# A four-stage fp32 transformer kernel: its written-out order of units, and their PSUM banks, replaced by another order and other banks

## The chip, the cores and the metric

One core of one Trainium2 chip. The metric is the device time in microseconds of one execution. The kernel before took 571.74, 571.04 and 569.04 us in three runs, median 571.04. All data is fp32.

## The reference

16 samples, each an image of 3 x 128 x 128 and a text of 32 tokens x 192. The image becomes 64 patches of 16 x 16 (768 numbers) and these tokens of 192. Three parts follow; `_layernorm` is without gain where none is given.

```python
# part 1, 64 image tokens per sample
x = layernorm(patches @ patch_w + patch_b) * g + b + positions
identity = x
x = sparse_attn(ff(x)) + identity        # ff = gelu(y @ ff1) @ ff2 (192 -> 768 -> 192); 12 heads of 16, window 64
x = ff(x) + x
h = concatenate([x, txt], axis=1)        # 96 tokens per sample
# part 2, y = layernorm(h)
y = y + (silu(conv4(xb)) * silu(z)) @ out_proj      # xb, z = halves of ln(y) @ in_proj
y = y + attn(ln(y)) @ attn_proj                     # 12 heads of 16 over 96 tokens
y = y + gelu(ln(y) @ ffn1) @ ffn2
h = h + y
# part 3, y = layernorm(h)
q, k, v = y @ qkv                        # 12 heads of 64, q and k normalised per head
o = softmax(q k / 8) v * gate(y)         # gates: 2 shared and 10 experts, the 2 highest kept
return h + o @ proj
```

## The kernel before, in words

The 16 samples are taken in 4 groups of 4. A group's 256 image tokens are 2 tiles of 128, its 384 tokens of all kinds are 3. The work of a group is cut into three chains, each a sequence of units: **a** is part 1 and the first branch of part 2 (the convolution), **b** is attention and feed-forward of part 2, **c** is part 3. Chain a of group 0 has buffers of its own and is written **d**; chain c of group 2 likewise, written **e**. A unit is one product of TensorE and what the other engines do with it. `STEPS_TEXT` (lines 70 to 103) names all 403 units in the order in which they are issued, as `name.k:group=bank`: `b_s.0:3=2` is the scores of the first sample set of group 3, in PSUM bank 2 and the two behind it. Some names that the text uses below:

- a_em: patches times weights (24 matmuls; needs x_in, a 768 KB load by SyncE, L623 for group 1, L643 for groups 2 and 3). a_x0: its transpose. a_f1 and a_f2: feed-forward, gelu on ScalarE (L1253). a_qk, a_v, a_s, a_pt, a_o, a_ot, a_pr: attention. a_in, a_cv, a_gt, a_out: the convolution branch, a_cv and a_gt without TensorE.
- b_u: transpose of the normalised tokens; its statistics are DVE's, the inverse root GpSimd's (L1931), the result `u` DVE's (L1611). b_qk, b_v: q, k and v. b_s: scores; DVE takes the maximum (L1715) and subtracts it, ScalarE takes the exponential (L1366, L1371). b_pt: the transposed probabilities, after DVE has divided (L1729, L1741). b_o, b_pr: the rest of attention. b_f1, b_f2: feed-forward.
- c_g: the gates (some 25 small DVE instructions). c_qk: q and k of one tile, normalised per head on DVE (L1828 to L1839) and GpSimd (L1983). c_qt: their transposes. c_v, c_s, c_pt, c_o, c_pr as in b.
- b_e, b_n, a_e, c_e, c_n and the like are parts of a softmax on ScalarE and DVE, without TensorE. a_bc, a_tb, a_pb and a_wc prepare biases and one weight. warm.0 to warm.3 are matmuls whose result nobody reads (L1220).

`run` (L527) goes through the order once per engine: TensorE, ScalarE, DVE and GpSimd each issue their part of every unit in the order of the text, and SyncE the loads of a_em and of the text of a_ht. So the place of a unit in the text is its place in each of these queues. There is no other planner.

PSUM has 8 banks. `BANKS` (L124) gives the number of neighbouring banks of each kind of unit: 3 for a_f1, a_in, b_qk, b_s, b_pt, b_f1, c_qk, c_qt, c_s and c_pt, 2 for a_qk, a_s, a_pt, b_u, b_v, c_v and c_o, 1 for the others. `PsumPlaces` (L165) takes the bank of the text where one is given (173 units before), and else the banks that have gone unused for longest. `reads_before` (L507) makes TensorE wait ahead of a unit until all that was in its banks has been read, by the counts in `READ_BY` (L129):

```python
"b_s": lambda k: [("b_sub", 3 * k + 3), ("b_exp", 2 * k + 1)],   # L129 ff.
```

Every wait on data is ahead of the unit's first matmul too:

```python
pe.wait_ge(w.S["x_in"], w.upto("x_in", w.a))                     # a_em, L774 ff.
for sem_read, value in reads_before(w, ("a_em", 0)):
    pe.wait_ge(sem_read, value)
```

`narrow_first_units` (L189) decides from the order for 23 units in which sequence their wide and narrow matmuls come; it gives 23 units with either text.

## Time and profile before

| | |
|---|---|
| three runs, us | 571.74, 571.04, 569.04 |
| profiled execution, span, us | 569.6 |
| TensorE busy (PE) | 515.9 us, 91%, 4673 matmuls |
| weight loads (PEld) | 396.6 us, 70% |
| VectorE busy (DVE) | 406.6 us, 71%, 891 instructions |
| ScalarE busy (ACT) | 299.0 us, 52%, 488 instructions |
| GpSimd busy (POOL) | 97.0 us, 17%, 85 instructions |
| DMA | 16.02 MB, nearly all in the first 60 us |

The span is the time from the first to the last instruction of one profiled execution, here 569.6 us, the execution's own time as far as the profile gives one; the three runs lie at most 2.1 us above it and 0.6 below. PE, DVE, ACT, POOL and SP are the five engines; PEld are the weight loads, which run beside the matmuls. "Granted clock" or PEclk is TensorE's clock as a share of 2.4 GHz.

### The profile page before, as it was taken

The numbers are of one execution on the slowest core, as the hardware profiler recorded it, in microseconds if no ns is written. First come the engines' busy times: TensorE is split into PE (matmuls) and PEld (weight loads), VectorE is DVE, ScalarE is ACT, GpSimd is POOL, SyncE is SP. The second block draws the span as 40 slices with busy tenths as digits, with TensorE's granted clock in tenths as the row PEclk, the third lists the DMA queues.
The fourth block names the chain that finished last, engine by engine and source line by source line (L and its number), as shares of the span: only waits on it lengthen the run. The fifth ranks groups of instructions, "written<-read, shape, count | busy, mean of one in ns | idle before, by whom it ended". The sixth has DMA issues, their size and how long they took to land.

```text
span 569.6 us, 11352 instructions
## 1 busy us (share of the span) xinstructions
PE 515.9 (91%) x4673; PEld 396.6 (70%) x4673; DVE 406.6 (71%) x891; ACT 299.0 (52%) x488; POOL 97.0 (17%) x85
## 2 busy tenths in 40 slices
PE   5799989898999999999999999999969798989696
PEld 5576667677887566786976667777945677686475
DVE  4234877688777957779768857869749688748982
ACT  0125446356338546858346546866335568525762
POOL 6022400100320422110010422100010231011200
PEclk9799999979999999999999999999998999999999
DMA  9995020000000000100000000000000000000000
GB/s 215 287 203 142 17 63 0 8 2 2 0 2 1 2 1 2 57 8 2 1 22 1 3 1 0 1 1 1 2 22 1 1 2 2 1 22 1 1 1 22
DMA packets 12675, 16.02 MB, mean 28 GB/s; under 512 B 6235, under 2 KB 10048, under 8 KB 12240
## 3 DMA queue, kind: packets, MB, share of 16 engines
q1 hardware_dynamic: 9712, 12.71, 9.4%
q10 hardware_dynamic: 2400, 2.00, 1.1%
q0 software_dynamic: 512, 0.59, 0.6%
q8 instruction: 37, 0.61, 0.5%
q14 instruction: 14, 0.11, 0.1%
HBM read 14.11 MB, written 1.18 MB: 27 GB/s over the span
## 4 chain that ended last, share of the span: by engine, by line
PE 70%; DVE 17%; ACT 7%; issue 3%; POOL 1%; DMA 1%; ACTq 0%; DVEq 0%; POOLq 0%
PE ps L692 16%; PE ps L1005 9%; PE ps L702 8%; PE ps L682 7%; PE ps L825 4%; PE ps L783 3%; DVE smax L1715 3%; DVE pr L1741 3%; PE ps L1066 2%; PE ps L1180 2%; DVE psum L1729 2%; PE ps L1202 2%; PE ps L1156 2%; PE ps L1056 2%; PE ps L840 2%
## 5 line engine op out<-in xcount | busy, mean ns | idle before, releaser
L1715 DVE TENSOR_REDUCE smax<-ps 96x12 f32<-96x1152 f32 (+1 forms) x28 | 37.8, 1351 | 18.1 <-PE ps L1056 10.8
L1729 DVE TENSOR_REDUCE psum<-pr 128x12 f32<-128x1152 f32 (+1 forms) x24 | 32.3, 1344 | 4.3 <-ACT pr L1371 4.3
L1366 ACT ACTIVATE pr<-ps,less 128x96 f32<-128x96 f32 (+1 forms) x96 | 24.6, 337 | 17.9 <-DVE less L1717 17.8
L1409 ACT ACTIVATE squares<-ps 128x1536 f32<-128x1536 f32 x12 | 17.4, 1450 | 27.5 <-PE ps L702 21.6
L1957 POOL TENSOR_TENSOR side_wide<-attn,w_mask 128x1024 f32<-128x1024 f32 (+1 forms) x12 | 20.7, 1748 | 59.1 <-ACT attn L1261 47.4
L1828 DVE TENSOR_REDUCE ss<-squares 128x24 f32<-128x1536 f32 x12 | 21.0, 1749 | 12.1 <-ACT squares L1409 12.1
L1983 POOL TENSOR_TENSOR squares<-squares,qk_root 128x512 f32<-128x512 f32 x8 | 16.7, 2082 | 75.0 <-DVE qk_root L1504 75.0
L1931 POOL TENSOR_TENSOR ln_root<-ln_root,minus_half 128x3 f32<-128x3 f32 x8 | 6.8, 856 | 129.5 <-DVE ln_root L1603 129.5
L682 PE MATMUL ps<-w_cqkv,side_c 64*96 64x384 f32 (+1 forms) x96 | 27.4, 500 | 0.0
L1005 PE MATMUL ps<-w_ff,b_kB 128*128 128x192 f32 x144 | 25.5, 329 | 0.0
L692 PE MATMUL ps<-w_cqkv,side_c 128*128 128x512 f32 (+1 forms) x72 | 25.0, 492 | 0.0
L1005 PEld LDWEIGHTS ps<-w_ff,b_kB 128*128 128x128 f32 x144 | 23.2, 190 | 0.5 <-issue 0.2
L1253 ACT ACT_TABLE_LOAD x7 | 9.0, 1283 | 26.6 <-PE ps L702 26.5
L1720 DVE TENSOR_TENSOR pr<-ps,smax 128x768 f32<-128x768 f32 (+1 forms) x24 | 22.8, 949 | 0.0
L1076 PE MATMUL ps<-w_ident,pr 128*96 128x128 f32 x144 | 18.0, 275 | 3.8 <-issue 2.4
L1376 ACT ACTIVATE side_qk<-ps 96x1536 f32<-96x1536 f32 x12 | 17.2, 1444 | 7.6 <-PE ps L1076 7.5
L1371 ACT ACTIVATE pr<-pr 128x768 f32<-128x768 f32 (+1 forms) x24 | 20.4, 852 | 0.0
L1076 PEld LDWEIGHTS ps<-w_ident,pr 128*96 128x96 f32 x144 | 15.2, 126 | 6.9 <-issue 3.9
L1005 PE MATMUL ps<-w_cproj,b_kB 128*128 128x192 f32 x108 | 19.3, 329 | 0.7 <-ACT b_kB L1441 0.7
L1056 PE MATMUL ps<-b_kB,heads 32*32 32x192 f32 x576 | 15.8, 360 | 4.6 <-ACT b_kB L1345 3.1
L692 PEld LDWEIGHTS ps<-w_cqkv,side_c 128*128 128x128 f32 x72 | 13.0, 190 | 9.9 <-issue 9.3
L1931 POOL TENSOR_TENSOR x_root<-x_root,minus_half 128x6 f32<-128x6 f32 (+1 forms) x6 | 6.5, 1091 | 73.9 <-DVE x_root L1606 37.5
(360 smaller groups left out, 1356.8 us busy)
## 6 DMA issues: line engine op xcount, KB each, us to landing
x_in<-in_xT SPq DMA_DIRECT2D x3, 768.0 KB, 4.5
b_kB<-in_cqkv SPq DMA_DIRECT2D x1, 1152.0 KB
w_cqkv<-in_cqkv SPq DMA_DIRECT2D x1, 864.0 KB
out<-side_c ACTq DMA_DIRECT2D x3, 288.0 KB, 2.3
w_cqkv<-in_cqkv SPq DMA_DIRECT2D x1, 855.0 KB
heads<-in_xT ACTq DMA_DIRECT2D x3, 256.0 KB, 3.8
side_in<-in_patchT SPq DMA_DIRECT2D x3, 192.0 KB, 4.4
side_tok<-in_tok_ff SPq DMA_DIRECT2D x2, 288.0 KB, 6.9
```

What stands on the lines that cost most here:

```text
L682: m = pe.matmul(out_ap, lhs(n, kc, r), rhs(n, kc, r), start=opens and banks[n] not in banks[:n], stop=closes and banks[n] not in banks[n + ...
L692: m = pe.matmul(out_ap, lhs, rhs, start=opens and bank not in [x[0] for x in wide[:n]], stop=closes and bank not in [x[0] for x in wide[n ...
L702: m = pe.matmul(out_ap, lhs(half, r), rhs(half, r), start=opens and part == 0, stop=closes and part == 1)
L825: m = pe.matmul(t[:, 0:TA], w_tff2[:, kc, 0:128], w.x.a_h[:, kc, :], start=(n == 0), stop=(n == F // 128 - 1))
L1005: m = pe.matmul(t[:, 0:D], lhs[:, kc, tile * 128:(tile + 1) * 128], rhs[:, kc, :], start=(kc == 0), stop=(kc == n_k - 1))
L1056: m = pe.matmul(t[32 * of:32 * of + 32, bank, second * 2 * N:(second + 1) * 2 * N], b_qT[r, c, at:at + 32], b_kBv[r, :, c, of * N:(of + 1) ...
L1076: m = pe.transpose(t[0:N, h // 4, h % 4 * 128:(h % 4 + 1) * 128], pr_all[:, s % 2, h * N:(h + 1) * N], w_ident[:, :])
L1366: m = act.activation(e[:, s % 2, h * N:(h + 1) * N], t[0:rows, h // 4, h % 4 * N:(h % 4 + 1) * N], ACT.Exp, scale=head ** -0.5, bias=less[ ...
L1715: dve.tensor_reduce(mx, t, AX.X, ALU.max).then_inc(w.S[stage + "_sub"], 1)
L1720: dve.tensor_tensor(e[:, s % 2, 0:DVE_LESS * N].rearrange("p (b h k) -> p b h k", b=b, k=N), t[:, 0:b], mx[:, 0:b].unsqueeze(3).to_broadca ...
L1729: dve.tensor_reduce(psum[0:rows, s % 2, :], e, AX.X, ALU.add).then_inc(w.S[done], 1)
L1828: dve.tensor_reduce(ss[:, :], sq.rearrange("p (h d) -> p h d", d=HD2), AX.X, ALU.add)\
```

## The change

Only the text of the order changes. It names the same 403 units, in another order, and 307 of them have a bank where 173 had. The whole text is replaced; these are the stretches of which the prediction speaks, in each of them the lines before (-) and after (+).

```diff
 STEPS_TEXT = """
-    d_en:0 d_em:0=7 a_bc=7 d_x0:0=7 d_f1.0:0=1 a_en:1 a_em:1=4 d_f2.0:0=5 d_h2.0:0=2 a_x0:1=4 d_qk:0=5 a_f1.0:1=2
-    d_v:0=6 d_e.0:0 d_s.0:0 a_f2.0:1=3 a_h2.0:1=6 d_pt.0:0 d_s.1:0 d_e.1:0 a_qk:1 d_o.0:0 d_pt.1:0=0 a_tb=5 d_ot.0:0
-    d_o.1:0 a_wc.0 warm.2 a_pb d_ot.1:0=2 a_e.0:1 d_pr:0=0 a_s.0:1=6 a_wc.1 d_f1.1:0=3 a_e.1:1 a_s.1:1=0 d_f2.1:0
-    d_h2.1:0 warm.1 d_ht:0=3 a_pt.0:1 a_v:1=6 a_o.0:1 d_u:0 a_pt.1:1 a_wc.2 d_in.0:0=2 a_ot.0:1 a_o.1:1=1 a_ot.1:1=7
...
-    d_out.1:0=7 d_out.2:0 a_f2.1:1=1 a_h2.1:1=5 b_u.1:0=3 a_ht:1 b_qk:0 a_u:1 b_e.0:0 b_s.0:0 b_s.1:0 b_e.1:0 b_v:0
-    b_n.0:0 b_n.1:0 a_in.0:1 b_pt.0:0=3 b_s.2:0 b_e.2:0 b_n.2:0 b_pt.1:0=3 a_in.1:1 b_pt.2:0=3 b_o.0:0 b_o.1:0=0
-    b_o.2:0=3 b_o.3:0=7 a_cv.0:1 a_cv.1:1 a_cv.2:1 a_gt.0:1 a_gt.1:1 b_pr.0:0=3 a_gt.2:1 b_pr.1:0 b_pr.2:0=2
-    a_em:2=0 a_out.0:1 a_out.1:1=1 b_u.2:0 a_out.2:1 b_f1.0:0=1 a_en:2 b_f1.1:0 b_u.1:1 a_wc.3 a_x0:2 b_f2.0:0
...
-    a_gt.0:2 c_pr.0:0 c_o.2:0=5 c_pt.3:0 a_gt.1:2 a_cv.2:2 c_pr.1:0=4 c_o.3:0=5 a_gt.2:2 a_out.0:2=7 a_out.1:2=1
-    a_out.2:2=4 a_em:3=3 b_u.1:2=5 a_en:3 c_pr.2:0=7 c_u:1 b_qk:2 b_v:2=6 a_x0:3 b_s.0:2=2 b_s.1:2 b_e.0:2 b_n.0:2
-    b_e.1:2 b_n.1:2 warm.3 a_f1.0:3 a_f2.0:3 a_h2.0:3=7 b_pt.0:2=1 b_s.2:2 b_e.2:2 b_n.2:2 a_qk:3=2 a_v:3=0 c_g:1=1
...
-    a_out.0:3=3 a_out.1:3=0 a_out.2:3=3 e_u:2=4 c_pr.2:1=3 b_u.1:3 b_qk:3=1 b_s.0:3=2 b_s.1:3 b_n.0:3 b_e.0:3 b_v:3
-    b_e.1:3 e_v.0:2=3 b_n.1:3 b_pt.0:3 b_s.2:3 b_e.2:3 b_n.2:3 e_qk.0:2=5 b_pt.1:3 b_pt.2:3 b_o.0:3=6 b_o.1:3
-    b_o.2:3 b_o.3:3 b_pr.0:3 b_pr.1:3=5 b_pr.2:3 e_v.1:2=0 e_g:2=4 b_u.2:3=0 e_qt.0:2 e_qk.1:2 e_qk.2:2=5 b_f1.0:3
...
-    c_v.0:3 c_qt.0:3=2 c_qt.1:3 c_s.0:3=0 c_e.0:3 c_s.1:3=5 c_n.0:3 c_e.1:3 c_n.1:3 c_qt.2:3 c_v.1:3=3 c_pt.0:3
...
+    d_en.0:0 d_em.0:0=3 warm.2:0=7 warm.1:0=2 a_bc.0:0=1 d_x0.0:0=5 a_em.0:1=7 d_f1.0:0=2 a_en.0:1 a_x0.0:1=0
+    d_f2.0:0=1 d_h2.0:0=7 a_f1.0:1=4 d_qk.0:0=1 a_f2.0:1=0 a_h2.0:1=1 d_e.0:0 d_s.0:0=6 d_v.0:0=5 a_qk.0:1=0 d_s.1:0=2
+    d_pt.0:0=4 d_e.1:0 d_o.0:0=0 d_pt.1:0=2 a_tb.0:0=4 d_ot.0:0=1 d_o.1:0=3 d_ot.1:0=7 a_pb.0:0=0 d_pr.0:0=6 a_e.0:1
+    a_s.0:1=0 a_wc.0:0 d_f1.1:0=3 a_e.1:1 a_s.1:1=0 d_f2.1:0=2 d_h2.1:0=3 warm.0:0=0 warm.3:0=4 d_ht.0:0=1 a_v.0:1=0
...
+    a_pr.0:1=4 d_gt.0:0 d_cv.1:0 d_cv.2:0 a_em.0:2=3 d_gt.1:0 d_gt.2:0 a_f1.1:1=4 a_en.0:2 d_out.0:0=0 d_out.1:0=7
+    d_out.2:0=3 a_f2.1:1=4 a_h2.1:1=2 b_u.1:0=6 a_ht.0:1=1 b_qk.0:0=5 a_u.0:1=1 b_e.0:0 b_s.0:0=4 b_s.1:0=0 b_e.1:0
+    b_n.0:0 b_n.1:0 a_in.0:1=5 b_pt.0:0=3 b_s.2:0=0 b_e.2:0 b_v.0:0=4 a_in.1:1=1 b_pt.1:0=5 b_n.2:0 b_pt.2:0=0
+    a_cv.0:1 a_cv.1:1 b_o.0:0=4 b_o.1:0=2 a_gt.0:1 a_gt.1:1 a_cv.2:1 a_gt.2:1 b_o.2:0=4 b_o.3:0=5 b_pr.0:0=1
+    b_pr.1:0=6 b_pr.2:0=7 a_out.0:1=1 a_out.1:1=7 b_u.2:0=4 a_x0.0:2=3 a_out.2:1=2 a_wc.2:0 b_f1.0:0=5 b_f1.1:0=0
...
+    b_pt.2:1=0 a_pt.1:2=5 c_g.0:0=7 b_o.0:1=6 b_o.1:1=1 b_o.2:1=2 b_o.3:1=0 b_pr.0:1=5 c_qt.0:0=2 c_qt.1:0=5
+    b_pr.1:1=0 b_pr.2:1=1 c_v.1:0=2 a_ot.0:2=6 a_o.1:2=1 b_u.2:1=2 a_ot.1:2=4 c_s.0:0=5 c_s.1:0=1 a_pr.0:2=0
+    a_em.0:3=7 c_n.0:0 c_e.0:0 c_e.1:0 c_n.1:0 a_en.0:3 c_qk.2:0=0 a_f1.1:2=4 b_f1.0:1=0 b_f1.1:1=5 a_f2.1:2=1
...
+    a_out.0:2=5 a_out.1:2=2 a_out.2:2=5 c_pr.2:0=3 b_u.1:2=5 a_x0.0:3=2 b_qk.0:2=4 a_f1.0:3=0 c_u.0:1=3 a_f2.0:3=7
+    b_s.0:2=1 b_e.0:2 a_h2.0:3=0 b_n.0:2 c_qk.0:1=5 c_qk.1:1=0 a_qk.0:3=4 b_v.0:2=6 b_pt.0:2=0 b_s.1:2=3 b_s.2:2=0
+    b_e.1:2 a_v.0:3=5 b_e.2:2 b_n.1:2 b_n.2:2 c_v.0:1=3 a_s.0:3=5 b_pt.1:2=0 a_e.0:3 c_g.0:1=7 b_pt.2:2=2 a_s.1:3=0
+    a_pt.0:3=5 b_o.0:2=2 b_o.1:2=5 b_o.2:2=7 a_e.1:3 b_pr.0:2=6 b_pr.1:2=5 b_o.3:2=4 a_o.0:3=6 a_pt.1:3=4 c_qt.0:1=0
...
+    a_out.2:3=2 e_u.0:2=6 c_pr.2:1=2 b_u.1:3=0 e_g.0:2=7 b_qk.0:3=2 e_qk.0:2=5 e_qk.1:2=2 b_v.0:3=0 e_qt.0:2=5
+    b_s.0:3=0 b_s.1:3=3 b_n.0:3 b_e.0:3 b_e.1:3 b_n.1:3 e_v.0:2=6 e_v.1:2=0 e_qt.1:2=2 b_pt.0:3=5 b_s.2:3=0 b_e.2:3
+    b_n.2:3 e_qk.2:2=4 b_pt.1:3=0 b_pt.2:3=5 e_s.0:2=0 b_o.0:3=7 e_s.1:2=3 e_n.0:2 e_e.0:2 b_o.1:3=7 e_e.1:2 e_n.1:2
...
+    c_g.0:3=6 c_qk.0:3=3 c_qk.1:3=0 c_qk.2:3=5 c_qt.0:3=1 c_qt.1:3=5 c_s.0:3=0 c_e.0:3 c_s.1:3=5 c_v.0:3=3 c_e.1:3
...
     """
```

A unit written without `.k` or with `.0` is the same unit.

## Rows read from the trace of the kernel before

**Rows 1.** The page, part 1: TensorE, busy us, share, instructions.
```profile
PE 515.9 (91%) x4673; PEld 396.6 (70%) x4673; DVE 406.6 (71%) x891; ACT 299.0 (52%) x488; POOL 97.0 (17%) x85
```

**Rows 2.** The page, part 4: the chain that ended last, by engine.
```profile
PE 70%; DVE 17%; ACT 7%; issue 3%; POOL 1%; DMA 1%; ACTq 0%; DVEq 0%; POOLq 0%
```

**Rows 3.** Windows: length, busy us of PE, PEld, DVE, ACT, POOL; PEclk; DMA share; GB/s.
```profile
17.47:24.30 6.83, 5.72 (x15) 4.45 (x16) 0.92 (x3) 0.00 (x0) 0.00 (x0) 0.50 1.09 268
...
113.05:119.87 6.82, 6.82 (x110) 5.08 (x89) 5.43 (x8) 4.63 (x12) 0.00 (x0) 0.50 0.01 2
...
427.07:430.48 3.41, 3.41 (x20) 2.33 (x12) 3.34 (x6) 1.76 (x5) 0.00 (x0) 0.50 0.00 0
```

**Rows 4.** The same view, stages between two starts.
```profile
75.78:112.84 37.06, 33.18 (x262) 25.59 (x263) 27.33 (x74) 16.89 (x30) 3.49 (x3) 1.00 0.10 27
...
186.00:235.00 49.00, 45.32 (x410) 33.14 (x410) 35.46 (x93) 28.00 (x37) 16.80 (x10) 1.00 0.06 18
...
281.32:345.00 63.68, 60.13 (x621) 44.78 (x621) 46.20 (x108) 32.45 (x56) 14.34 (x11) 1.00 0.02 6
...
416.50:456.00 39.50, 30.89 (x382) 22.30 (x383) 26.87 (x50) 20.09 (x34) 2.94 (x2) 0.96 0.03 9
...
456.00:509.71 53.71, 49.85 (x454) 40.27 (x454) 41.35 (x95) 32.90 (x50) 9.32 (x6) 1.00 0.01 2
...
509.71:569.60 59.89, 48.33 (x427) 35.24 (x425) 42.32 (x94) 31.40 (x46) 6.24 (x3) 1.00 0.03 11
```

**Rows 5.** One source line, the load of x_in: issue and landing.
```profile
L623 SPq DMA_DIRECT2D x_in<-in_xT x1: 432/432/432, 10.3 to 10.3; - x1
...
DMA to landing us min/median/max: 12.2/12.2/12.2
```

**Rows 6.** Timeline: start, length, engine, line, operation [idle before <-releaser]; PE, the start.
```profile
18.28 0.42 PE L745 MATMUL ps<-w_ident,squares 128*128 128x128 f32 x1
...
26.22 4.17 PE L783 MATMUL ps<-side_in,x_in 128*128 128x192 f32 x24
...
30.22 1.03 PE L825 MATMUL ps<-side_qk,side_tff 128*128 128x256 f32 x4
```

**Rows 7.** Timeline, PE: the wide part of a_f1.0:3.
```profile
299.40 2.83 PE L692 MATMUL ps<-x0T,side_tok 128*128 128x256 f32 x12 [0.82 <-ACT pr L1366]
```

**Rows 8.** Timeline, ACT: the gelu table behind d_f1.0.
```profile
26.46 1.28 ACT L1253 ACT_TABLE_LOAD   x1 [26.46 <-PE ps L702]
```

**Rows 9.** Timeline, 112 to 146 us, PE, ACT and DVE.
```profile
112.84 3.37 PE L1056 MATMUL ps<-b_kB,heads 32*32 32x192 f32 x96 [1.36 <-DVE b_kB L1705]
...
116.29 1.04 ACT L1366 ACTIVATE pr<-ps,less 128x96 f32<-128x96 f32 x4 [1.61 <-DVE less L1717]
...
123.22 1.47 PE L1076 MATMUL ps<-w_ident,pr 128*96 128x128 f32 x12
...
140.54 4.06 PE L783 MATMUL ps<-side_in,x_in 128*128 128x192 f32 x24
...
144.58 0.96 DVE L1611 TENSOR_SCALAR u<-pT,ln_mv,ln_root 128x192 f32<-128x192 f32 x3 [0.96 <-POOL ln_root L1931]
```

**Rows 10.** Timeline, 282 to 286 us, PE and DVE.
```profile
282.29 4.06 PE L783 MATMUL ps<-side_in,x_in 128*128 128x192 f32 x24
...
284.83 0.96 DVE L1611 TENSOR_SCALAR u<-xr,x_mv,x_root 128x192 f32<-128x192 f32 x3 [0.96 <-POOL x_root L1931]
```

**Rows 11.** Timeline, PE, b_s and b_v of group 3.
```profile
425.18 2.34 PE L1056 MATMUL ps<-b_kB,heads 32*32 32x192 f32 x96 [2.66 <-ACT b_kB L1345]
...
427.45 3.79 PE L682 MATMUL ps<-w_qkv,bT 128*96 128x192 f32 x16
```

**Rows 12.** Timeline, DVE in the tail: c_g, c_qk and the first maximum.
```profile
513.03 0.20 DVE L1775 TENSOR_REDUCE gsm<-ps 96x4 f32<-96x40 f32 x1 [1.72 <-PE ps L682]
...
518.68 1.75 DVE L1828 TENSOR_REDUCE ss<-squares 128x24 f32<-128x1536 f32 x1
...
534.18 1.35 DVE L1715 TENSOR_REDUCE smax<-ps 96x12 f32<-96x1152 f32 x1 [0.17 <-PE ps L1180]
```

More of the change, by code:

```diff
@@ L81 @@
-    a_h2.0:2 b_pt.0:1 b_s.2:1 a_v:2 b_n.1:1 b_e.2:1 a_qk:2=6 c_v.0:0=1 b_n.2:1 c_g:0 b_pt.1:1=3 b_pt.2:1=0 a_s.0:2=6
-    b_o.0:1=2 b_o.1:1=3 b_o.2:1=4 b_o.3:1 a_e.0:2 a_s.1:2=2 a_pt.0:2 b_pr.0:1=4 b_pr.1:1 a_e.1:2 a_o.0:2 a_pt.1:2=2
-    b_pr.2:1=6 a_ot.0:2=3 a_o.1:2=2 c_qk.0:0=4 a_ot.1:2=0 c_qk.1:0=1 a_pr:2=6 c_qt.0:0=3 c_qk.2:0 a_f1.1:2=3
-    c_qt.1:0 a_f2.1:2=7 b_u.2:1=4 a_h2.1:2 c_s.0:0=3 c_s.1:0 c_n.0:0 c_e.0:0 c_v.1:0 c_e.1:0 c_n.1:0 b_f1.0:1
-    b_f1.1:1=0 a_ht:2 b_f2.0:1=7 c_pt.0:0 b_f2.1:1=6 c_qt.2:0=2 a_u:2 b_f2.2:1 c_o.0:0=1 c_pt.1:0=3 c_s.2:0 c_e.2:0
@@ L91 @@
-    a_e.1:3 b_o.3:2=0 a_o.0:3=7 a_pt.1:3=1 b_pr.2:2 a_ot.0:3=5 a_o.1:3=6 c_qk.0:1 a_ot.1:3 c_qk.1:1=5 c_v.0:1 a_pr:3
-    c_qt.0:1=4 c_qk.2:1 a_f1.1:3 c_qt.1:1=0 a_f2.1:3=6 b_u.2:2 c_s.0:1=0 c_s.1:1 a_h2.1:3=3 c_n.0:1 c_e.0:1 c_e.1:1
-    b_f1.0:2=0 b_f1.1:2 c_n.1:1 a_ht:3 c_qt.2:1 c_v.1:1 c_pt.0:1 a_u:3 b_f2.0:2=5 c_o.0:1 c_pt.1:1 c_s.2:1 c_e.2:1
-    c_s.3:1=0 c_e.3:1 c_n.2:1 c_v.2:1=6 c_n.3:1 a_in.0:3=3 b_f2.1:2=0 c_o.1:1=4 c_pt.2:1 c_v.3:1=4 a_in.1:3 a_cv.0:3
-    a_cv.1:3 a_cv.2:3 c_pr.0:1 a_gt.0:3 b_f2.2:2=0 a_gt.1:3 c_o.2:1=6 c_pt.3:1=2 c_pr.1:1=5 a_gt.2:3 c_o.3:1
@@ L105 @@
+    c_o.1:3=1 c_e.3:3 c_v.3:3=3 c_pr.0:3=1 c_pt.2:3=4 c_o.2:3=6 c_pt.3:3=0 c_n.3:3 c_pr.1:3=5 c_o.3:3=6 c_pr.2:3=1
     """
```

25 lines of the change are left out of this document (16 added, 9 removed).

## The prediction, made before the changed kernel ran

> **What bounds the kernel now.** I read the page from the top. TensorE is busy for 515.9 of 569.6 us, 91%, and the chain that ended last lies on it for 70% of the span, on VectorE for 17% [rows 1, 2]. So the time is TensorE's work plus its holes, 569.6 - 515.9 = 53.7 us, plus what a lower clock adds inside the busy time. The granted clock is at its lower level (0.50, which is 1.2 GHz) in three stretches, 17.06 us in all: 17.47 to 24.30, 113.05 to 119.87 and 427.07 to 430.48 us [rows 3]. The windows then tell where the holes are [rows 4]: 3.88 us in 75.78 to 112.84 (37.06 less 33.18), 3.68 in 186 to 235, 3.55 in 281 to 345, 8.61 in 416.5 to 456, 3.86 in 456 to 509.71 and 11.56 in the tail. In the tail VectorE is busy for 42.32 of 59.89 us and takes the maximum only 0.17 us after its last work [rows 4, 12]: there it is VectorE that sets the pace.
>
> The change leaves every matmul in place, so 515.9 us stay but for the clock. What can change is the cover of each wait: how much TensorE work stands between a product and the next unit that needs its result back from ScalarE, VectorE, GpSimd or a DMA. I went through the new order unit by unit with the durations and latencies of before. The sum goes against the profiled execution's 569.6 us, which is 1.4 us under the median 571.04; I add the difference to the median.
>
> **A, the start (15 to 76 us): +3.0 us.** The new order puts a_em of group 1 ahead of d_f1.0. It reads x_in, whose DMA is issued at 10.3 us and takes 12.2 us, so it lands at 22.5 [rows 5]. TensorE is at that point when d_x0 ends, 18.28 + 0.42 = 18.7 us, where before a_em came at 26.22 without a wait [rows 6]. From 22.5: a_em 4.06 (its length at full clock [rows 10]), then d_f1.0 of 2.83 us for its wide part [rows 7] and 1.5 for the narrow one, end 30.9. Then ScalarE must load the gelu table, 1.28 us [rows 8], and make the first tile, 0.5, and only a_x0 (0.6) stands in between: d_f2.0 starts near 32.9 where it started at 30.22 [rows 6], +2.7. The clock: before, TensorE was near idle from 13.84 until the fall at 17.47. Now 1.6 us of warm matmuls stand in that hole, but two holes follow, so I expect a stretch at half clock over a_em as well: at most the 6.83 us of before [rows 3], adding between 0 and 2.5 us; I take 1.3. Against it go the warm matmuls, moved into a hole (-1.6), and the 0.9 us wait ahead of d_qk. d_o.0 and d_ot.1 now stand directly behind d_pt.0 and d_o.1: +1.5. Sum 2.7 + 1.3 - 1.6 - 0.9 + 1.5 = 3.0, from 1.6 to 4.3.
>
> That d_f1.0 can't slip past a waiting a_em: in the trace every matmul behind a wait starts after it [rows 9, 11]. The Trainium skill ("TensorE: Matmul & The Clock Gate", Part 2, Step-by-step) says the same, only weight loads are pulled ahead; if matmuls could pass, A would be about -1. The Trainium skill's page "DMA: Bandwidth & Descriptors" (Specifications) gives about 358 GB/s per core; here the load stretch shows 268 GB/s with the DMA engines all busy [rows 3]. By the page x_in would land, as an estimate, a quarter sooner (near 17 us), there would be no stall, and A would be about -1 too; the trace has the landing itself, so I keep 22.5.
>
> **B (76 to 112): -0.8 us.** a_em of group 2 comes here, as cover ahead of a_f1.1, and two warm matmuls cover d_ht. Of 3.88 us of holes [rows 4] I see about 0.8 covered; bounds -1.5 and -0.2.
>
> **C (112 to 148): +3.0 us.** First, a_in.0:1 is placed in banks 5 to 7, and b_s.0:0 in 4 to 6. So it waits until the exponentials of b_s.0:0 have been read: the first four end at 116.29 + 1.04 = 117.33, b_s itself ends at 112.84 + 3.37 = 116.21, and the last follow within a microsecond [rows 9]. +1.2 to 1.9. Then b_pt.0:0 has only a_in.0 (3.3) where b_v stood as well; it started at 123.22, 7.0 us after b_s ended [rows 9], and now would have 1.5 + 3.3 = 4.8 us plus b_s.1's own part: +1.0. Second, a_em:2 stood at 140.54 for 4.06 us [rows 9] between b_pr and b_u.2, whose input u comes at 144.58 + 0.96 = 145.54 off GpSimd's root [rows 9]. b_pr ended as a_em began; a_out.0 and a_out.1 give 2.1 us of cover. 145.5 - 140.5 - 2.1 = 2.9, and the gates that a_out needs are as late: +3.2. Third, b_v and a_in.1 now stand between b_s.2, b_pt.1 and b_pt.2, where 1.7 us of holes were: -1.4. VectorE works on during the first stall, so part of the second is paid: -1.4. 2.6 + 3.2 - 1.4 - 1.4 = 3.0; from 1 (the clock doesn't fall, b_v is 1.8 us shorter) to 5.
>
> **D (148 to 235): -0.7 us.** 3.68 us of holes in 186 to 235 [rows 4]; in the new order c_qk and c_v stand between b's and a's softmax units and I count about 3 left, with one new bank handover (c_qt.1:0 in bank 5 behind b_pr.0:1). From -3 (all gone) to +0.5.
>
> **235 to 281: 0.** 0.3 us of holes before; nothing to gain.
>
> **E (281 to 345): +2.2 us.** a_em:3 stood at 282.29 for 4.06 us with u ready at 284.83 + 0.96 [rows 10]. It is moved 45 us ahead. a_out.2 to b_u.1 took 3.7 us and 2.1 remain as cover: +1.6, b_qk:2 +0.5. Two handovers (a_v:3 in bank 5 behind b_s.1:2, a_o.0:3 in 6 behind b_pr.0:2) cost up to 1.5 and 1.4 by the exponentials' latency above; I take half, +1.5. Of the 3.55 us of holes [rows 4] 1.4 go. From 0 to +4.
>
> **F (345 to 416.5): -0.9 us.** The smallest term: two TensorE waits, 0.3 us ahead of b_f1.0:2 and 1.2 ahead of c_qt.2:1, get a unit before them; from -2.2 to 0.
>
> **G (416.5 to 509.71): -3.9 us.** Before, b:3 runs with little beside it: b_s.0:3 waits 2.66 us, and b_v behind it, from 427.45, runs for 3.03 of its 3.79 us at half clock, which costs half of that, 1.5 [rows 3, 11]. The new order puts e_g, e_qk.0 and e_qk.1 (9.7 us of matmuls) ahead of b_s.0:3. Gone: 2.66, 1.5 of clock, 0.9 ahead of b_pt.0, and 1.5 each ahead of b_pt.2 and b_o.0, 8.1 together. New: VectorE takes 518.68 - 513.03 = 5.65 us for c_g and (534.01 - 518.68) / 3 = 5.1 for each c_qk [rows 12], so 15.9 us for e_g and two e_qk, while TensorE has 18 us of work until b_s.0:3 ends, so the maximum starts hardly late; later stages with e_s, e_pt and e_o lose cover, and I count 4.2. Bounds: -7 (half of the 12.5 us of holes and the clock) and +3 (rival 2).
>
> **Tail: 0 +- 0.3.** c_v.0:3 moves behind c_s.1:3. VectorE has no hole there [rows 12], so a TensorE hole that is filled gives nothing back.
>
> **Sum.** 3.0 - 0.8 + 3.0 - 0.7 + 0 + 2.2 - 0.9 - 3.9 + 0 = +1.9. Profiled: 571.5; on the median 572.9 us. What a measurement of this kernel tells from no change is 0.5%, 2.9 us; so this is "within 0.5%", just.
>
> **Rivals.**
> 1. *The cover is spread better than my gap count shows* (0.31). G gives -7, D -3, F -2, and A and C stay at their lower ends, 1.6 and 1: with B -0.8 and E +2.2 the sum is -8.0, 563.0 us; with half of those differences about 568. For it: the largest holes, in 416 to 456 [rows 4], get 9.7 us of matmuls, and a clock that doesn't fall there. Against: units that lose cover in C and E.
> 2. *VectorE becomes the bound in b:3* (0.15). It takes its units in the same order, and e_g's and two e_qk chains stand ahead of b_s.0:3's maximum. If they take over the 18 us that TensorE has (the root and the products on GpSimd come back late), b's softmax, the longest chain of G, starts late by all of it, and TensorE stands at b_pt.0:3. It decides from 18 us on; at 22 us G is about +3 and the sum +8.8: 579.8 us.
> 3. *The start at half clock and the lost covers at their upper ends* (0.2): A 4.3, C 5, E 4: sum +7.3 on top of G -3.9 and the rest as above less 0.4, 578 us.
> 4. *Banks decide nothing and stalls move only* (part of my forecast, 0.34): TensorE's holes after are as many as before, in other places. That the kernel does other work than before is excluded: the same 403 units, the same shapes.
>
> My range for 8 in 10: 563 to 581, which takes in rival 1's end and rival 2. The likeliest one alone spans 569 to 576. Chances from the cases: faster by over 0.5% 0.31, within 0.5% 0.34, slower by over 0.5% 0.35 (rivals 2 and 3).
>
> **What would show it.** A: a hole before a_em:1 that ends at 22.5 with x_in's DMA named, and d_f2.0 near 32.9 or later. C: a hole at a_in.0:1 released by ScalarE's exponentials, and one ahead of b_u.2:0 released by DVE u. E: a hole of 1 to 2 us ahead of b_u.1:2. G: no clock fall near 427 and b_s.0:3 without a wait; a maximum that starts over 2 us after it would be rival 2. I am wrong if A shows no wait for x_in, if 416 to 510 keeps 12 us of holes, or if new waits come in D to F that are not named here.

## The result, and the profile after

The changed kernel takes 585.14 us (584.68 to 585.30 in four runs) where the kernel before, beside it, took 571.39: a ratio of 1.0237 (95%: 1.0193 to 1.0281), slower by 13.7 us. The forecast was 572.9 us, 563 to 581; the time lies outside that range.

The first view is part 1 and part 4 of the page (they answer to [rows 1, 2]). All line numbers are 3 higher than before, as the text of the order is 3 lines longer (in most runs below they are 4 or 5 higher).

```profile
PE 522.7 (90%) x4673; PEld 400.4 (69%) x4673; DVE 404.9 (69%) x891; ACT 293.8 (50%) x484; POOL 95.7 (16%) x85
...
PE 57%; DVE 23%; issue 8%; ACT 5%; POOL 3%; DMA 2%; SPq 2%; ACTq 0%; DVEq 0%; POOLq 0%
```

TensorE's busy time has grown by 6.8 us (522.7 less 515.9) with the same 4673 matmuls, and the span by 13.6 (583.2 less 569.6), so the holes have grown by 6.8 as well. The chain lies on TensorE for 57% of the span where it was 70%, on VectorE for 23% where it was 17%, and 8% of it is "issue", time in which the engine waited for nothing that the profile shows.

Where in the span that lies is shown by windows cut at the same two units in both kernels, the starts of b_u.1:3 and of c_u:3 (before, then the changed kernel; the tail of before is the last line of [rows 4]):

```profile
0.00:416.54 416.54, 386.87 (x3416) 298.82 (x3416) 296.09 (x654) 214.60 (x358) 78.47 (x74) 0.98 0.15 36
416.54:509.71 93.17, 80.74 (x833) 62.56 (x834) 68.19 (x144) 52.99 (x84) 12.26 (x8) 0.98 0.02 5
```

```profile
0.00:426.43 426.43, 386.73 (x3416) 298.07 (x3416) 294.47 (x654) 210.91 (x355) 77.22 (x74) 0.97 0.14 35
426.43:520.00 93.57, 83.66 (x833) 63.77 (x834) 68.05 (x144) 49.98 (x82) 12.21 (x8) 0.96 0.02 5
520.00:583.20 63.20, 52.33 (x427) 38.60 (x425) 42.37 (x94) 32.92 (x47) 6.24 (x3) 0.92 0.03 10
```

Up to b_u.1:3 the loss of 9.9 us is holes alone (29.7 us before, 39.7 after). Behind it the holes have shrunk, by 2.5 us in G and 0.7 in the tail, and TensorE's busy time has grown, by 2.9 and 4.0 us.

The second view, windows (columns as in [rows 3]), shows the lower clock that goes with the longer busy time. The granted clock is at its lower level in six stretches, 41.0 us in all, where [rows 3] has three and 17.06:

```profile
14.97:25.28 10.31, 4.76 (x16) 4.31 (x17) 1.24 (x6) 0.00 (x0) 0.00 (x0) 0.50 1.07 274
...
120.91:127.73 6.82, 4.87 (x12) 3.23 (x14) 6.68 (x10) 3.53 (x10) 0.00 (x0) 0.50 0.00 1
...
328.93:335.75 6.82, 4.23 (x34) 3.21 (x35) 6.72 (x8) 2.89 (x8) 2.34 (x2) 0.51 0.01 4
...
427.93:434.76 6.83, 6.83 (x31) 5.33 (x31) 4.22 (x20) 0.92 (x2) 0.00 (x0) 0.51 0.14 46
...
523.58:527.00 3.42, 3.42 (x13) 2.24 (x10) 2.66 (x15) 0.25 (x1) 0.00 (x0) 0.51 0.00 0
...
540.84:547.66 6.82, 5.77 (x50) 5.40 (x52) 5.52 (x14) 3.20 (x4) 3.08 (x2) 0.51 0.00 1
```

Here and below, a fall is the clock going from its upper to its lower level. The end of the last unit that both orders have in common at a point gives what each stretch costs. I took the units' ends from both traces and set 4.06 us off wherever an a_em has moved from one stretch to another:

The prediction parted E and F at 345 us; the two traces are parted at 365.

| stretch (time before) | predicted | by the two traces |
|---|---|---|
| A, start to d_h2.1:0 | +3.0 | +1.7 |
| B, 76 to 112 us | -0.8 | -0.1 |
| C, 112 to 148 | +3.0 | +4.9 |
| D, 148 to 281 | -0.7 | -0.6 |
| E, 281 to 365 | +2.2 | +5.5 |
| F, 365 to 416.5 | -0.9 | -1.3 |
| G, 416.5 to 510 | -3.9 | +0.4 |
| tail | 0 | +3.3 |
| sum | +1.9 | +13.8 |

Now the places, in timelines (columns as in [rows 6]). The start, which answers to [rows 6]:

```profile
21.86 5.83 PE L786 MATMUL ps<-side_in,x_in 128*128 128x192 f32 x24 [5.01 <-DMA x_in<-in_xT]
...
33.78 1.56 PE L828 MATMUL ps<-side_qk,side_tff 128*128 128x256 f32 x6 [1.40 <-ACT side_qk L1256]
```

a_em.0:1 waits 5.0 us for x_in and takes 5.83 at half clock for most of it; d_f2.0 starts 3.6 us later than in [rows 6]. Stretch C, to be read beside [rows 9]:

```profile
122.86 4.18 PE L695 MATMUL ps<-xlT,side_in 128*128 128x384 f32 x8 [2.04 <-ACT pr L1369]
...
126.28 1.36 DVE L1744 TENSOR_TENSOR pr<-pr,rec 128x1152 f32<-128x1152 f32 x1
...
128.59 1.26 ACT L1327 ACTIVATE attn<-ps 128x384 f32<-128x384 f32 x3 [2.93 <-PE ps L705]
...
130.00 1.49 PE L1079 MATMUL ps<-w_ident,pr 128*96 128x128 f32 x12 [1.45 <-ACT attn L1327]
...
148.26 0.59 PE L671 MATMUL ps<-w_proj,heads 97*128 97x192 f32 x2 [1.15 <-ACT heads L1391]
...
152.65 0.33 PE L747 MATMUL ps<-w_ident,u 128*128 128x128 f32 x1 [0.86 <-DVE u L1614]
```

The holes are where they were forecast: 2.0 us for the exponentials in a_in.0:1's bank, 1.45 ahead of b_pt.0:0, and 1.15 and 0.86 where a_em:2 is missing. But the one ahead of b_pt.0:0 isn't the softmax that was forecast: the divided probabilities are there at 126.28 + 1.36 = 127.64 us. The line names ScalarE's copy of a_in.0:1 out of PSUM (L1327), done at 129.85. b_pt.0:0 has banks 3 to 5 and a_in.0:1, right ahead, has 5 to 7, so this is a second handover of a bank. Stretch E, whose rows of before are [rows 10], three engines:

```profile
325.53 1.28 PE L1059 MATMUL ps<-b_kB,heads 32*32 32x192 f32 x48
...
327.44 1.35 DVE L1718 TENSOR_REDUCE smax<-ps 128x12 f32<-128x1152 f32 x1
...
328.39 2.89 POOL L1960 TENSOR_TENSOR side_wide<-attn,w_mask 128x1024 f32<-128x1024 f32 x2
...
328.83 1.48 DVE L1720 TENSOR_SCALAR less<-smax 128x4 f32<-128x4 f32 x1
...
330.34 1.03 ACT L1369 ACTIVATE pr<-ps,less 128x96 f32<-128x96 f32 x4 [3.26 <-DVE less L1720]
...
331.52 3.02 PE L874 MATMUL ps<-side_tok,attn 128*64 128x96 f32 x32 [3.02 <-ACT pr L1369]
```

b_s.1:2 is done on TensorE at 325.53 + 1.28 = 326.81. Its maximum starts 0.6 us later, as VectorE has to finish the second of the two c_qk chains that stand ahead of it. Then `less` (L1720), 0.17 us elsewhere, takes 1.48 beside GpSimd's mask product for a_qk:3, which started 0.44 ahead of it. The exponentials, and with them the bank that a_v.0:3 wants, are free at 331.4, 4.6 us behind b_s.1. TensorE waits 3.0 us, and the clock falls inside that hole. Stretch G and the tail, beside [rows 11, 12]:

```profile
447.47 1.53 PE L1159 MATMUL ps<-w_ident,squares 128*128 128x128 f32 x12 [1.46 <-POOL squares L1986]
...
451.51 1.35 DVE L1718 TENSOR_REDUCE smax<-ps 128x12 f32<-128x1152 f32 x1
...
459.23 1.52 PE L1079 MATMUL ps<-w_ident,pr 128*96 128x128 f32 x12 [1.11 <-DVE pr L1744]
...
469.67 1.49 PE L1079 MATMUL ps<-w_ident,pr 128*96 128x128 f32 x12 [1.54 <-ACT squares L1415]
...
530.68 1.75 DVE L1831 TENSOR_REDUCE ss<-squares 128x24 f32<-128x1536 f32 x1 [1.60 <-ACT squares L1412]
...
541.89 2.82 PE L1159 MATMUL ps<-w_ident,x_in 128*128 128x128 f32 x12 [3.27 <-POOL x_in L1986]
...
544.64 3.67 PE L1183 MATMUL ps<-side_qk 64*96 64x96 f32 x48
...
546.93 1.35 DVE L1718 TENSOR_REDUCE smax<-ps 96x12 f32<-96x1152 f32 x1 [0.92 <-PE ps L1183]
```

In G the wait of 2.66 us ahead of b_s.0:3 has gone, and e_qt.0 waits 1.46 for GpSimd instead, b_pt.0:3 1.11 where 0.89 was, b_pt.2:3 1.54 where 1.49 was. In the tail c_qt.1:3 waits 3.27 us for GpSimd; c_v.0:3, which filled 2.3 us of that, is gone. c_qt.1:3 and both c_s then run at half clock (3.67 us for two c_s of 1.3), and the maximum, 0.17 us behind VectorE's last work in [rows 12], is 0.92 behind.

### The profile page after: what moved, and what is told of

Same layout as the page of the kernel before. It is cut to its first block, busy times and chain, and to the rows that moved or that the text cites. A ratio compares the mean times of both kernels' runs of the same rounds, so it can differ in the third digit from the quotient of the medians.

```text
span 583.2 us, 11360 instructions
## 1 busy us (share of the span) xinstructions
PE 522.7 (90%) x4673; PEld 400.4 (69%) x4673; DVE 404.9 (69%) x891; ACT 293.8 (50%) x484; POOL 95.7 (16%) x85
## 4 chain that ended last, share of the span: by engine, by line
PE 57%; DVE 23%; issue 8%; ACT 5%; POOL 3%; DMA 2%; SPq 2%; ACTq 0%; DVEq 0%; POOLq 0%
PE ps L695 13%; PE ps L1008 7%; PE ps L705 7%; PE ps L685 6%; PE ps L828 3%; DVE ss L1831 3%; DVE smax L1718 2%; PE ps L1183 2%; PE ps L1205 2%; PE ps L1069 2%; DVE psum L1732 2%; PE ps L888 2%; DMA x_in<-in_xT 2%; PE ps L1159 2%; PE ps L786 2%
## 5 line engine op out<-in xcount | busy, mean ns | idle before, releaser
L685 PE MATMUL ps<-w_cqkv,side_c 128*96 128x384 f32 (+1 forms) x96 | 28.4, 515 | 0.0
L1960 POOL TENSOR_TENSOR side_wide<-attn,w_mask 128x1024 f32<-128x1024 f32 (+1 forms) x12 | 19.5, 1648 | 32.5 <-PE ps L888 18.3
L695 PE MATMUL ps<-xlT,side_in 128*128 128x384 f32 (+1 forms) x64 | 19.3, 451 | 2.0 <-ACT pr L1369 2.0
L1008 PE MATMUL ps<-w_cproj,b_kB 128*128 128x192 f32 x108 | 19.4, 330 | 0.8 <-ACT b_kB L1444 0.8
L1008 PEld LDWEIGHTS ps<-w_cproj,b_kB 128*128 128x128 f32 x108 | 17.5, 190 | 1.8 <-ACT b_kB L1444 0.9
```

What stands on the lines that cost most here:

```text
L685: m = pe.matmul(out_ap, lhs(n, kc, r), rhs(n, kc, r), start=opens and banks[n] not in banks[:n], stop=closes and banks[n] not in banks[n + ...
L695: m = pe.matmul(out_ap, lhs, rhs, start=opens and bank not in [x[0] for x in wide[:n]], stop=closes and bank not in [x[0] for x in wide[n ...
L1008: m = pe.matmul(t[:, 0:D], lhs[:, kc, tile * 128:(tile + 1) * 128], rhs[:, kc, :], start=(kc == 0), stop=(kc == n_k - 1))
L1960: pool.tensor_tensor(w.x.a_kB[0:rows, heads_of, :], w.x.a_kT[0:rows, c, t2 * 128:(t2 + 1) * 128].unsqueeze(1).to_broadcast(shape), w_mask[ ...
```

## The experiments

All are changes of the order's text alone. "Old" is the text before, "new" the changed one. In a hybrid each unit has the bank that it has in the text it comes from; a seam is a place where it passes from one text to the other. Ratios are against the kernel before on the same chip, with their 95% interval.

### One stretch of the new order in the old one

```diff
 s_start: new up to d_h2.1:0, old behind
 s_mid:   old to d_h2.1:0, new to a_h2.1:3 (75 to 365 us), old behind
 s_b3:    old to b_u.1:3, new to b_f2.1:3 (419 to 500 us), old behind
 s_tail:  old to c_u:3, new behind
-    c_qk.2:3 c_v.0:3 c_qt.0:3 c_qt.1:3 c_s.0:3 c_s.1:3
+    c_qk.2:3 c_qt.0:3 c_qt.1:3 c_s.0:3 c_s.1:3 c_v.0:3
```

> The new order and banks up to d_h2.1:0 (with all four warm units' new places kept where that stretch has them), the old ones behind it. In the two traces the stretch ends 1.7 us later than in the kernel before. Theory 1 (losses are local and add up): +1.7 us, with TensorE waiting for x_in until about 22 us and the clock at half around 15 to 25 us. Rival (a later wait swallows what the start loses): 0 +- 0.5. Rival 2 (a clock fall later in the kernel depends on the start's phase): more than +3 or less than 0, with the half-clock stretches of 113 and 427 us gone or others added.

Measured: 582.29 against 571.14, 1.0190 (1.0156 to 1.0224), +11 us: Theory 1 missed by far. At d_h2.1:0 the trace is 1.8 us late, as expected. The rest comes behind it. a_wc.1, 4.0 us of VectorE work that scales a weight, had come to stand ahead of d_ht's statistics at the seam, and TensorE waits for what is behind it; timeline of this run, VectorE and TensorE:

```profile
78.36 1.42 DVE L1876 TENSOR_SCALAR b_kB<-b_kB,ones_row 128x2304 f32<-128x2304 f32 x1
...
79.81 2.56 DVE L1879 TENSOR_TENSOR w_cqkv<-w_cqkv,b_kB 128x2304 f32<-128x2304 f32 x1
...
82.92 0.90 DVE L1597 BATCH_NORM_STATS2 e_small<-ps 128x6 f32<-128x192 f32 x3
...
86.14 1.50 PE L914 MATMUL ps<-side_wide,attn 128*64 128x34 f32 x24 [4.39 <-ACT side_wide L1278]
```

> The new order and banks from d_h2.1:0 to a_h2.1:3 alone (75 to 365 us), the old ones on both sides. From the two traces this stretch holds +9.5 us of the 13.6. Theory 1 (local): +9.5 us, with TensorE waits at a_in.0:1 (about 2), b_pr.1:0 (1), a_v.0:3 (3) and half-clock stretches near 115 and 320 us. Rival (the loss comes of the banks that meet at the seams or of state carried from the start): below +5.

Measured: 584.38, 1.0224 (1.0191 to 1.0258), +13.2. In its trace the stretch costs 11.6 us, 1.2 of it at a seam ahead of b_f1.0:2, with the same holes as in the changed kernel, a_v.0:3's 3.03 among them. So the stretch is worth about 10, as forecast; what the time has on top came behind it, in half-clock stretches over the old b:3.

> The new order and banks from e_g to b_f2.1:3 alone (419 to 500 us), the old ones on both sides. From the two traces +0.4 us, where the prediction had -3.9. Theory 1 (local): +0.4 +- 1, with a half-clock stretch of 6.8 us right behind e_g. Rival (the stretch would be worth -3 and lost it only because the clock fell in the changed kernel by the phase it came in with): -2 to -4 us, and no clock fall at e_g.

Measured: 570.65, 0.9995 (0.9972 to 1.0019): no gain to be seen, as in Theory 1. But in this trace the clock fell at 420 us for 3.4, so it doesn't test the rival, which needs a trace without a fall. Others below have none.

> The old order up to c_u:3, the new one behind it: c_v.0:3 behind c_s.1:3, c_pt.2:3 behind c_v.3:3, other banks. The changed kernel lost 3.3 us here, 1.7 of it in a half-clock stretch over c_qk.0:3 that the move can't have caused. Theory 1 (the hole of 3.3 us ahead of c_qt.1:3 halves the clock over c_qt.1 and c_s and delays DVE's maximum): +1.6 us, half clock from about 527 to 534 us. Rival (VectorE sets the pace, as predicted): 0 +- 0.3. Rival 2 (the order makes the first fall too): +3.3.

Measured: 571.35, 1.0005 (0.9981 to 1.0028), an interval from -1.1 to +1.6 us, which leaves Theory 1 its edge and can't tell. The trace has the mechanism, and from c_u:3 to the end it takes 61.6 us, 1.7 more than in the kernel before. That is no more than the old order takes there when a fall of 3.4 us comes near its start (61.6 in before_2, s_b3, s_f and others), so the trace can't tell either:

```profile
527.70 2.82 PE L1160 MATMUL ps<-w_ident,x_in 128*128 128x128 f32 x12 [3.27 <-POOL x_in L1987]
...
532.74 1.35 DVE L1719 TENSOR_REDUCE smax<-ps 96x12 f32<-96x1152 f32 x1 [0.91 <-PE ps L1184]
```

### One repair inside the new order

```diff
 m_start
-    d_x0 a_em.0:1 d_f1.0:0
+    d_x0 d_f1.0:0 a_em.0:1
 m_c1 (banks old as well)
-    b_s.0:0=4 b_s.1:0=0 a_in.0:1=5 b_pt.0:0 b_s.2:0 b_v:0 a_in.1:1 b_pt.1:0 b_pt.2:0
+    b_s.0:0=0 b_s.1:0=5 b_v:0=3 a_in.0:1=0 b_pt.0:0 b_s.2:0 b_pt.1:0 a_in.1:1 b_pt.2:0
 m_e: old order behind b_u.1:2 up to a_h2.1:3, so
-    b_s.0:2 a_h2.0:3 c_qk.0:1 c_qk.1:1 a_qk:3 b_v:2 b_pt.0:2 b_s.1:2 b_s.2:2 a_v:3 c_v.0:1
+    b_s.0:2 b_s.1:2 a_f1.0:3 ... b_pt.0:2 b_s.2:2 a_qk:3 a_v:3 c_g:1 ... a_o.1:3 c_qk.0:1 a_ot.1:3 c_qk.1:1
 nopin_after: every "=bank" taken out
```

> The changed kernel with one unit moved: a_em.0:1 behind d_f1.0:0 again, banks kept. Theory 1 (at the start the only loss is that a_em waits for x_in with d_f1 behind it): d_f1.0 starts near 18 us, a_em finds x_in landed, d_f2.0:0 starts near 30 where it started at 33.8 in the changed kernel: -3.8 us against it, +9.9 against the kernel before. Rival (the clock, at half over this stretch in both, takes it back): -1 to -2 against the changed kernel.

Measured: 585.72, 1.0223 (1.0172 to 1.0274), nothing gained in the median, though the times spread from 578.87 to 586.00. In the profiled one (585.88) a_em no longer waits, but a_x0.0:1, right behind it, does, 3.35 us, and d_f2.0 starts at 32.7: the stall follows the chain a_em, normalisation, a_x0, which the new order has too close either way. Both theories had missed that unit.

> The changed kernel with the old order and banks of the units from b_s.0:0 to b_pt.2:0 (b_v.0:0 ahead of a_in.0:1, a_in.1:1 behind b_pt.1:0, b_s in banks 0 to 2 and 5 to 7, b_v in 3 and 4). Theory 1 (a_in.0:1 waits for the bank of b_s.0:0, and b_pt.0:0 lacks cover): the holes of 2.0, 1.45 and 0.4 us go, those of 0.2, 1.2 and 0.2 of the kernel before come back: -2.4 us against the changed kernel, +11.3 against before; b_pr.1:0 and b_u.2:0 keep their holes of 1.15 and 0.9. Rival (the later holes grow as VectorE isn't given time to catch up, as the prediction priced with 1.4 us): -1.0.

Measured: 583.13, 1.0216 (1.0174 to 1.0257), 2.0 us under the changed kernel; the size fits Theory 1, the intervals overlap. Up to b_u.1:3 its trace is 1.5 us ahead of the changed kernel's. Its later holes (1.16 and 0.87) haven't grown, one of 0.85 ahead of b_o.2 is new.

> The changed kernel with the old order and banks of the units behind b_u.1:2 up to a_h2.1:3 (so c_qk.0:1 and c_qk.1:1 stand behind a_o.1:3 again); a_em.0:3 stays 45 us ahead, where the change put it. Theory 1 (VectorE's two c_qk chains stand ahead of the maximum of b_s.1:2, and a_v.0:3 waits for b_s.1:2's bank): the hole of 3.0 us ahead of a_v.0:3 and the clock fall behind it go: -4 us against the changed kernel, +9.6 against before. Rival (the stage's loss is mostly the missing cover of a_em.0:3, as the prediction had it): -1 or less.

Measured: 581.19, 1.0182 (1.0147 to 1.0218), 4.0 us under the changed kernel, the size of Theory 1, but not where it had it. The hole ahead of a_v.0:3 is gone; a_f1.0:3 has one of 1.78 and other small ones are new, so that from b_u.1:2 to a_u:3 the trace takes 91.8 us, where the changed kernel takes 90.6, and b_u.1:3 starts 0.4 us later. All of the gain comes behind that, where nothing was edited: the clock did not fall at e_g and b_qk:3, where the changed kernel has the fourth of its six stretches, though the units there, their order and the holes ahead of them are the same. Windows of this run:

```profile
428.10:435.00 6.90, 6.90 (x43) 5.11 (x44) 5.03 (x25) 2.90 (x6) 0.00 (x0) 1.00 0.14 45
```

> The new order without any bank given: each unit takes the banks that have gone unused for longest. Of the new order's 307 TensorE units 103 share a bank with one of the two units before them; without given banks 35 do (80 in the kernel before). Theory 1 (the order makes the loss, banks only name the unit that waits): within 2 us of the changed kernel, +12 to +15 against before, with the hole ahead of a_v.0:3 moved to a neighbour. Rival (bank handovers cost several microseconds by themselves): 3 us or more faster than the changed kernel, under +10.5 against before.

Measured: 588.57, 1.0293 (1.0249 to 1.0337), 3.4 slower than the changed kernel. The rival is dead; the intervals overlap, so that it is slower is likely and not shown. a_in.0:1 waits 1.98 us as before, b_pt.2:2 now 1.98, a_s.0:2 3.15. And b_pt.0:0, with banks 3 to 5 where a_in.0:1 now has 0 to 2, starts without a wait at the end of a_in.0:1, in the same order of units:

```profile
128.86 1.51 PE L1074 MATMUL ps<-w_ident,pr 128*96 128x128 f32 x12
```

So the hole of 1.45 us of the changed kernel was the shared bank 5, and not missing cover. As a whole the given banks don't hurt the new order.

### Restoring, filling, repeating

```diff
 fix_all: new, but old order and banks of b_s.0:0 to b_f1.1:0 with
-    d_cv.2:0 a_em:2 a_f1.1:1 ... b_pr.2:0 a_out.0:1
+    d_cv.2:0 a_f1.1:1 ... b_pr.2:0 a_em:2 a_out.0:1
 and of the stretch of m_e, and of all behind c_u:3
 before_warm: old, with ten more units
+    d_em warm.4 a_bc warm.5 warm.6 d_x0 ... a_u:1 warm.7 b_s.0:0 ... b_pt.1:0 warm.8 a_in.1:1 b_pt.2:0 warm.9
+    c_pr.2:1 warm.10 b_u.1:3 warm.11 b_qk:3 warm.12 warm.13 b_s.0:3
```

> The changed kernel with three stretches in the old order and the old banks: b_s.0:0 to b_f1.1:0 (a_em.0:2 back behind b_pr.2:0 as well), the units behind b_u.1:2 up to a_h2.1:3 (a_em.0:3 stays early), and all behind c_u.0:3. The start, 76 to 112 us, group 1's stage and the stage of b:3 stay new. By the two traces those kept stretches are worth +1.7 (start), about 0, -0.2, +1.5 (b_u.1:2 and b_qk:2 without a_em:3), -1.3 and +0.4. Theory 1 (the losses are local, and these three stretches hold nearly all): 573 to 575 us, +2 to +4 against before. Rival (seams and the phase of the clock decide as much as the order): +7 or more.

Measured: 586.78 against 571.31, 1.0263 (1.0227 to 1.0299): the rival, and more. Nothing came off, though each of the three stretches lost its holes. New ones opened where units had been taken away or met a foreign neighbour; the first is where a_em:2 had stood (the other large one, 1.48 us, is at 167.41):

```profile
102.12 2.24 PE L1009 MATMUL ps<-side_out,squares 128*128 128x192 f32 x10 [2.01 <-DVE squares L1674]
```

> The kernel before with ten more warm units (20 matmuls of 128 x 384 whose result nobody reads, 0.8 us a unit), each in a hole that the trace shows: three at the start, one ahead of each of b_s.0:0, a_in.1:1, b_o.0:0, b_u.1:3 and b_qk.0:3, two ahead of b_s.0:3. It is extra work, none of it on data that anybody waits for. Theory 1 (the clock falls because of these holes, and the half clock of 17 us costs some 6 us of TensorE time): the falls near 17, 113 and 427 us go and the time falls by 3 to 6 us, 565 to 568. Rival (the falls have another cause, such as units of few columns): no change within 1 us, the falls stay.

Measured: 570.68, 1.0001 (0.9976 to 1.0027): no gain. The clock near 113 us stayed at its upper level (the next run shows that it can without them). Where b_v runs at full clock, b_pt waits longer for VectorE; TensorE ahead of b_pt.0:3, where before it was 0.89:

```profile
436.88 2.37 PE L1081 MATMUL ps<-w_ident,pr 128*96 128x128 f32 x10 [2.47 <-DVE pr L1746]
```

What a half clock costs there is shown by the kernel before itself, whose second profile (below) has no fall at 113 us:

```profile
112.00 2.25 PE L1056 MATMUL ps<-b_kB,heads 32*32 32x192 f32 x96 [1.35 <-DVE b_kB L1705]
...
121.06 1.51 PE L1076 MATMUL ps<-w_ident,pr 128*96 128x128 f32 x12 [1.40 <-DVE pr L1741]
```

From b_s.0:0 to b_pt.0:0 it takes 9.06 us, and 10.38 with the fall [rows 9]. b_s and b_v are 2.9 us longer at half clock, so of these 1.3 reach b_pt.0:0 and the rest is hidden behind VectorE. The run doesn't show that the clock costs nothing, for the ten units are work too: TensorE's busy time is 522.3 us, 6.4 over before. Its profile is also of its slowest execution (575.42 us, mean granted clock 0.985). Seven of its twelve executions have a mean clock of 0.990 or more and take 568.56 to 570.71 us; the three at 0.985 take 573.60 to 575.42, some 3 us more than the kernel before at the same clock.

> The kernel before, unchanged, for another profile. Theory 1 (a given order has its given clock falls): half clock near 17, 113 and 427 us again and a span within 1 us of 569.6. Rival (with the same holes the fall comes or not by the execution): other stretches, another sum than 17 us.

> The changed kernel, unchanged, for another profile. Theory 1 (a given order has its given clock falls): half clock near 15, 121, 329, 428, 524 and 541 us again, 41 us in all. Rival: the falls without a large hole ahead of them (428, 524) are missing or last differently, those at the holes of 2 to 5 us (15, 121, 329, 541) are there again.

Measured: 571.49 and 586.55. Second profiles: spans of 569.7 and 584.7, mean clocks of 0.985 (as the first) and 0.962 (0.965 in the first). The sum of half-clock time comes back in the kernel before (17.1 us) and is 44.4 us for 41.0 in the changed one; the places come back only in part. Before the second time (windows): none at 104 to 122 us, where [rows 3] has 6.8 us, and one at 505 to 520 that was not there.

```profile
104.00:122.00 18.00, 14.78 (x181) 10.88 (x180) 14.96 (x30) 11.00 (x23) 1.32 (x1) 1.00 0.04 6
...
415.00:435.00 20.00, 15.33 (x200) 10.43 (x201) 12.11 (x16) 10.03 (x20) 0.00 (x0) 0.83 0.05 16
...
505.00:520.00 15.00, 13.41 (x72) 9.88 (x70) 6.95 (x28) 4.16 (x5) 0.34 (x1) 0.89 0.06 20
```

The changed kernel, second time: again at the start, near 121, 331, 430 and 543 us, a new one of 3.4 us near 455, but none at 520 to 530.

The record has the mean granted clock of every timed execution, and within one kernel the time follows it. These are the executions of the kernel before that were timed beside the experiments, 84 in all, the five clocks that have at least seven:

| mean granted clock | executions | median, us |
|---|---|---|
| 0.991 | 7 | 568.6 |
| 0.988 | 10 | 568.7 |
| 0.985 | 29 | 571.0 |
| 0.982 | 18 | 572.0 |
| 0.979 | 8 | 573.1 |

From 0.979 to 0.991 the half-clock time goes from some 24 to 10 us, and the time by 4.5. The four executions of the changed kernel are at 0.965 to 0.968.

### Each costly stretch alone, and what gains

```diff
 s_start2: s_start with a_wc.1 behind a_o.1:1 and d_ht:0=4
 s_c: old to d_h2.1:0, new to b_f1.0:0 (75 to 150 us), old behind
 s_e: old, new from c_pr.2:0 to a_h2.1:3 (282 to 365 us), with a_em:3 between c_s.0:0 and c_s.1:0
 s_f: old, new from a_h2.1:3 to b_u.1:3 (365 to 417 us)
 best: old, new from a_h2.1:3 to b_f2.1:3 (365 to 500 us)
 m_cet: new with the edits of m_c1, m_e and the old order behind c_u:3; a_em:2 and a_em:3 stay
```

> As the first start experiment (new order and banks up to d_h2.1:0, old ones behind), but a_wc.1 stands behind a_o.1:1, where the new order has it, and d_ht:0 has bank 4. In the first one a_wc.1, 4.0 us of VectorE work on a weight, had come to stand ahead of d_ht's statistics at the seam and made a hole of 4.4 us ahead of a_o.0:1. Theory 1 (the start by itself loses 1.7 us): +2 us against before. Rival (the new start costs more through what it leaves for later, clock falls among it): +5 or more.

Measured: 581.32 against 571.20, 1.0200 (1.0173 to 1.0227), +10.1. The rival. The profiled one (581.69) is 1.8 us late at d_h2.1:0, then 2.3 up to a_v.0:1, 1.9 at d_out.0:0, and more later: the old order behind doesn't fit what the new start leaves. It is holes and not clock: busy time is 515.5 us, as before, the holes 64.4 for 53.7.

> The new order and banks from warm.0:0 to b_f1.0:0 alone (75 to 150 us), the old ones on both sides. Theory 1 (this stretch holds +5 of the 13.6: holes of 2.0 ahead of a_in.0:1, 1.45 ahead of b_pt.0:0, 1.15 and 0.9 ahead of b_pr.1:0 and b_u.2:0): +4 to +5 us. Rival (holes move and another stage gives them back): under +2.

Measured: 583.83, 1.0201 (1.0161 to 1.0240), +11.5 by the ratio. Far over both. The times spread most here, from 578.23 us (mean clock 0.985) to 588.89 (0.959), and the profiled one took 587.11 (0.965). In its trace 4.4 us lie in the stretch itself, 2.2 at its seam (b_f1.1:0 shares banks with b_f1.0:0 right ahead).

> The new order and banks from c_pr.2:0 to a_h2.1:3 alone (282 to 365 us), a_em.0:3 between c_s.0:0 and c_s.1:0 as cover lost, the old order and banks elsewhere. Theory 1 (c_qk.0:1 and c_qk.1:1 ahead of b_s.1:2 keep VectorE from its maximum, a_v.0:3 waits 3.0 us for its bank): +5 us and one more at the seam ahead of b_f1.0:2 (1.5 for 0.3), +5 to +6. Rival (loss only by the clock's phase): +2 or less.

Measured: 581.89, 1.0205 (1.0175 to 1.0235), +10.7, where 5 to 6 were expected. The hole is the one of the changed kernel, 3.03 us, with the same stretched `less`, in an order that but for a_em:3 and a warm unit is the old one up to c_pr.2:0. The excess has a cause of its own, the first line here: c_v.1:0, with banks 6 and 7, stands close behind the inserted a_em:3 in bank 7 and waits 3.02 us, until VectorE has read that at 240.42. Before, there was no hole there:

```profile
240.53 3.87 PE L686 MATMUL ps<-w_cqkv,side_c 64*96 64x384 f32 x8 [3.02 <-issue]
...
323.31 1.35 DVE L1719 TENSOR_REDUCE smax<-ps 128x12 f32<-128x1152 f32 x1
...
324.26 2.89 POOL L1961 TENSOR_TENSOR side_wide<-attn,w_mask 128x1024 f32<-128x1024 f32 x2
...
324.70 1.48 DVE L1721 TENSOR_SCALAR less<-smax 128x4 f32<-128x4 f32 x1
...
327.39 3.02 PE L875 MATMUL ps<-side_tok,attn 128*64 128x96 f32 x32 [3.03 <-ACT pr L1370]
```

> The old order to a_h2.1:3, the new one from there to b_f2.1:3 (365 to 500 us), the old one behind. By the two traces 365 to 417 us gives -1.3 and 419 to 500 +0.2 to +0.4. Theory 1 (local effects add): -1 us, 570.2, which the measurement can hardly tell from none. Rival: +-0 or slower by a clock fall behind e_g.

Measured: 566.52, 0.9940 (0.9910 to 0.9970): 4.7 us faster than the kernel before by the medians (3.4 by the ratio), more than Theory 1's 1, and faster than both kernels. The gain goes with the clock. Eight of the twelve executions have a mean clock of 0.994 and take 565.46 to 567.85 us; two of the 84 of the kernel before have that. The three at 0.982 take 571.08 to 573.39, no less than the kernel before at 0.982. The trace is of one of these three (span 569.3 us), so it can't show which fall the others lack; in it, 365 to 417 takes 1.4 us less.

> The old order with the new one from a_h2.1:3 to b_u.1:3 alone (365 to 417 us). The hybrid with the new order from 365 to 500 us ran 4.7 us faster than the kernel before, the stretch of 419 to 500 alone changed nothing. Theory 1 (the gain is that of 365 to 417, two waits that go, 1.5 us, and fewer half-clock stretches): -1.5 to -4. Rival (only the two stretches together gain, the new order of b:3 needs the state that 365 to 417 leaves): 0 +- 1.

Measured: 570.71 against 570.40, 1.0021 (0.9991 to 1.0050): the rival, this part alone gains nothing that can be told. With s_b3's 0.9995 neither half of the best one gains by itself. The twelve executions of either have mean clocks of 0.976 to 0.991, none 0.994.

> The changed kernel with three repairs, each inside the new order and without taking a_em.0:2 or a_em.0:3 from where the change put them: the old order of b_s.0:0 to b_pt.2:0 (-2.0 alone), the old order behind b_u.1:2 up to a_h2.1:3 (-4.0 alone) and the old order behind c_u.0:3 (the traces: -3.3, timed alone in the other kernel 0.2). Theory 1 (repairs that leave the rest of the schedule in place add up): 6 to 9 us faster than the changed kernel, 576 to 579. Rival (holes only move, as when three longer stretches were restored): under 2 us gained, 583 or more.

Measured: 576.31 against 570.40, 1.0119 (1.0073 to 1.0164): 8.8 us under the changed kernel by the medians, 6.7 by the ratios, its interval clear of it. The size is Theory 1's. The page and the windows of this run:

```profile
PE 513.2 (89%) x4673; PEld 392.8 (68%) x4673; DVE 405.4 (71%) x891; ACT 295.8 (51%) x486; POOL 95.8 (17%) x85
...
0.00:424.21 424.21, 384.42 (x3416) 296.12 (x3416) 295.04 (x654) 213.04 (x357) 77.33 (x74) 0.98 0.14 35
424.21:514.54 90.33, 80.40 (x832) 61.42 (x833) 68.04 (x144) 50.04 (x82) 12.22 (x8) 1.00 0.02 5
```

The mechanism is not Theory 1's. The holes are 61.3 us in all, where the changed kernel has 60.5: those three went, and others opened, as the rival had it. Up to b_u.1:3, where two of the three repairs lie, only 2.2 us are gained. The rest is 3.2 us in G, where nothing was edited, and 3.2 in the tail, and all of it is busy time (9.5 us less): of the six stretches at half clock two are left, the start and one near 121 us.

## Why the prediction was wrong

What was right: the holes named for A (x_in), C and F are there, the terms of A, B, C, D and F are within 2 us, and the signs are right but for G and the tail. Two things failed. Up to b_u.1:3 the sum had +5.8 us, 1.3 of it clock, and the traces have +9.9, all of it holes: E and C. Behind it the sum had -3.9, 1.5 of it clock that was to come back, and the traces have +3.7: the holes shrank as forecast and the clock took it all.

**G, -3.9 forecast, +0.4 found.** The step that failed: "Gone: 2.66, 1.5 of clock, 0.9 ahead of b_pt.0, and 1.5 each ahead of b_pt.2 and b_o.0, 8.1 together". Without the clock the sum has 6.6 us of holes gone and 4.2 new, 2.4 less; found are 2.5 less. That is luck in part: of the holes named as gone only the 2.66 and 1.2 of b_o.0's went, and 1.3 of the 1.58 ahead of b_qk:3, which isn't in the sum. b_pt waits for VectorE's maxima and divisions, which come after b_s wherever it stands. The term that decided was the clock: it fell over e_g and b_qk:3, and instead of 1.5 us back TensorE's busy time grew by 2.9. The traces of this order of b:3 show what that is worth, for their holes in this stretch are 9.7 to 9.9 us:

| half clock within G, us | from b_u.1:3 to c_u:3, us | traces |
|---|---|---|
| 0 | 90.3 | m_e, m_cet, fix_all |
| 3.4 | 92.0 | m_c1, best |
| 6.8 | 93.6 | the changed kernel, m_start |
| 10.2 | 94.7 and 95.3 | the changed kernel again, nopin_after |

The old order takes 93.2 us with 3.4 of half clock and 93.8 with 6.8 (the two profiles of the kernel before). So where the clock stays up the new order of b:3 does gain, 2.8 us against the profile of before, and the forecast of -3.9 is about right; at equal clock it gains 1.2 or 0.3. Why it falls at e_g in some executions and not in others is open.

**E, +2.2 forecast, +5.5 found.** I priced the cover of a_em:3 (1.6 and 0.5; found 0.86 and 0.66) and gave the handover of a_v:3 "half" of 1.5. It was 3.0, and the clock fell in it (some 2.3 us more over a_v and c_v). Of the 3.0, by the timeline, 0.6 is VectorE's queue, with two c_qk chains ahead of the maximum (rival 2's mechanism, which I looked for only in G), and 1.3 is `less` stretched beside GpSimd; 1.1 is what the usual latency of some 2.8 us leaves (in the kernel before, from b_s.0:0's end near 114.5 us to 117.33). m_e takes all three away at once, s_e puts all three into the old order and has the same hole; no run parts them. Nor does a run show the 3.0 us come back: m_e lost the hole and none of the time up to b_u.1:3.

**The tail, 0 forecast, +3.3 found.** "VectorE has no hole there, so a TensorE hole that is filled gives nothing back": the move opened one of 3.27 us, and it reached VectorE through c_s, which came late. But the holes of the tail are 0.7 us fewer in all, and what it has on top is 10.2 us at half clock in two stretches, 4.0 us of busy time. The first comes ahead of the move and is missing in the second profile, whose tail is 1.3 us over before. The old order's tail is itself 59.9 us without a fall and 61.6 with one of 3.4. So the failed step is that the term left the clock out; what the move costs by itself isn't shown.

**C, +3.0 forecast, +4.9 found.** The first stall, 2.6 in the sum, is 2.04 + 1.45 = 3.5; the second, 3.2 less 1.4 for what VectorE makes good, is 1.15 + 0.86 = 2.0; the small holes gave 1.05 for 1.4. The first is the mis-sized term, and half of it had the wrong mechanism: "Then b_pt.0:0 has only a_in.0 (3.3) where b_v stood as well" prices missing cover for the softmax, and the wait is for bank 5, which b_pt.0:0 shares with a_in.0:1. The lines and nopin_after show it.

**A, +3.0 forecast, +1.7 found.** The wait for x_in is there, 5.0 us, and the half clock lasts 10.3 us where at most 6.8 were allowed for. The estimate of a landing near 17 us has a slip: a quarter off the 12.2 us of transfer gives 10.3 + 9.1 = 19.4 us, so a stall of 0.7 us would stand by it too. The landing taken from the trace, and with it the sum, is untouched. That matmuls keep their order agrees with the trace: d_f1.0 started only behind the waiting a_em, as in the Trainium skill ("TensorE: Matmul & The Clock Gate", Part 2, Step-by-step).

**The clock.** The sum had it at the start and in b:3, +1.3 and -1.5, -0.2 in all. Half-clock time went from 17 to 41 us, 6.8 us of busy time, half of the 13.6. Which stretches fall changes from one execution to the next; that more of them fall in the changed kernel comes back in both its profiles, and the mean clocks of all its timed executions say the same. No run changes the clock alone. But the same kernel is faster where it stayed up, and so is the same order of G, so it can't be set aside as a mere sign of the holes.

The cause as far as the runs bear it: 9.9 us of holes come up to b_u.1:3, at the places that the trace shows in A, C and E; behind it there are 3.2 us fewer holes and 6.9 us more busy time, the clock's. m_cet removes the holes at a_in.0:1, b_pt.0:0, a_v.0:3 and c_qt.1:3 and wins 6.7 to 8.8 us, nearly all of it clock; 7.7 of the 9.9 us up to b_u.1:3 are still lost in it, in holes that moved. For the start (1.7), the two holes where a_em:2 is missing (2.0) and the two where a_em:3 is (1.5) that is argued from the trace alone: given back in fix_all, a_em:2 left as large a hole where it had been. Banks as a whole are not it (nopin_after), though single holes are.

## What to carry to other kernels

Cover has to be counted on every queue: before moving a unit, list what the engine that answers it has ahead of the answer, for a moved unit brings its vector work along, GpSimd's too. Count PSUM banks of neighbouring units as waits as well. Where two orders are each packed tight, a piece of one in the other costs more at its seams than the piece is worth (+10.1, +11.5 and +10.7 us for three pieces that the two traces put at +1.7, +4.9 and +5.5). And after a repair look where the time came back: compare stretch by stretch, holes and busy time apart, and at the same half-clock time, from more than one execution. Two of the repairs here had the forecast size and gained it elsewhere.

## What the runs showed of the hardware

The same units with the same hole of 1.21 us ahead of b_u.1:3 ran at full clock in one execution and at half in another (427.93 to 434.76 us in the changed kernel, 428.10 to 435.00 in m_e). Over the stretch G, 3.4 us more of half clock went with some 1.6 us more of time (table above). Over whole executions of the kernel before, some 14 us more of it went with 4.5.

A VectorE instruction can be stretched by 1.0 to 1.3 us beside a wide GpSimd product: `less` on 128 x 4 took 1.48 instead of 0.17 beside L1960 (above). In the kernel before the same mask product's victim, at 316.36 us, was a division (L1741) of 2.36 instead of 1.36 that nobody waited for so closely. The Trainium skill, "SBUF — State Buffer" ("Who interferes with whom"), has VectorE and GpSimd share one pair of ports: an instruction of VectorE with two SBUF inputs contends with GpSimd's reads, and in a two-port mode, which tensor_scalar can enter, the one that comes second is blocked for the whole instruction of the other. The trace agrees: `less` is a tensor_scalar, started 0.44 us behind the first of the two products, which ran from 328.39 for 1.89 us, and ended 0.03 us behind it, at 330.31. So moving a unit can put this second onto a short instruction in a critical chain.

Differences of 3 us between two kernels want many executions, with their clocks: the best one's twelve run from 565.5 to 573.4 us, eight of them at a mean clock of 0.994 up to 567.9.
